# The vector engine's order of work in the last seven routing tiles of a gated attention and mixture-of-experts kernel

## What is computed

```python
x = x + tanh(g_xattn) * attention(layernorm(x), ctx)        # ... @ Wo.T + bo at its end
n = layernorm(x)
shared = (silu(g_s) * y_s) @ w_shared_down                  # g_s, y_s from n @ w_shared_up
scores = sigmoid(n @ w_gate)                                # 64 scores for each token
topk_idx = top 6 of scores; w = their scores, summed to 1
pos = running count of the tokens that chose the same expert before this one
routed = sum over the 6 of w * expert(n), where pos < 512
x = x + tanh(g_ffn) * (shared + routed)
```

## Time and profile before

| | before |
|---|---|
| median of three runs | 3068.83 us (3068.48 to 3069.22) |
| the profiled execution's own time | 3070.04 us |
| span of its trace | 3068.3 us |
| mean granted TensorE clock, as a share of full speed | 0.989 |
| busy: PE, DVE, ACT, POOL | 97%, 72%, 44%, 45% of the span |

### The profile page before, as it was taken

How to read it: one execution, slowest core, us unless ns; L and a number is a source line. 1 busy time by engine, 2 the same in 40 slices (tenths; PEclk the granted TensorE clock), 3 DMA queues, 4 the chain that set the end, 5 groups by cost and what they waited for, 6 DMA issues and landing times.

```text
span 3068.3 us, 62706 instructions
## 1 busy us (share of the span) xinstructions
PE 2981.7 (97%) x21264; PEld 1809.6 (59%) x21264; DVE 2205.3 (72%) x3798; ACT 1352.5 (44%) x2189; POOL 1388.5 (45%) x1325
## 2 busy tenths in 40 slices
PE   6999999999999998999999899999999999999997
PEld 5677777777777764444444445555555555555553
DVE  6677777778787777777777766666666666666664
ACT  5444444444454454111111125555555555555553
POOL 4222222221212213455555745666666665666664
PEclk9999999999999999999999999999999999999998
DMA  5333334333333336444445558999999998999995
GB/s 227 77 94 90 98 95 107 93 87 84 87 87 91 90 103 203 133 136 137 137 136 136 136 178 210 231 249 254 237 244 249 242 244 239 254 260 258 255 259 119
DMA packets 428876, 509.78 MB, mean 166 GB/s; under 512 B 234446, under 2 KB 332750, under 8 KB 428704
## 3 DMA queue, kind: packets, MB, share of 16 engines
q1 hardware_dynamic: 348832, 305.97, 33.3%
q0 software_dynamic: 79872, 201.48, 28.7%
HBM read 340.27 MB, written 201.79 MB: 177 GB/s over the span
## 4 chain that ended last, share of the span: by engine, by line
PE 90%; issue 4%; DVE 2%; POOL 1%; DMA 1%; ACT 0%; SPq 0%; another core or an unknown queue 0%; ACTq 0%; POOLq 0%; DVEq 0%
PE proj_ps L872 7%; PE eturn_ps L2128 7%; PE proj_ps L874 7%; PE proj_ps L873 7%; PE proj_ps L918 4%; PE proj_ps L920 4%; PE proj_ps L919 4%; PE v_ps L2138 3%; PE v_ps L2137 3%; PE v_ps L2139 3%; PE g_ps L2138 3%; PE g_ps L2139 3%; PE g_ps L2137 3%; PE edown_ps L2156 3%; PE edown_ps L2154 3%
## 5 line engine op out<-in xcount | busy, mean ns | idle before, releaser
L1924 POOL DMA_INDIRECT out<-outs,target x256 | 402.2, 1571 | 319.8 <-ACT outs L2015 260.9
L2038 DVE TENSOR_TENSOR ext_lo<-eturn_ps,ext_hi 128x1024 f16<-128x1024 f32 x254 | 311.0, 1224 | 260.9 <-ACT ext_hi L1975 252.3
L1891 POOL DMA_INDIRECT rows<-rows_dram,index x256 | 354.5, 1385 | 118.4 <-POOL index L1887 59.6
L1975 ACT ACTIVATE ext_hi<-eturn_ps 128x1024 f16<-128x1024 f32 x254 | 259.9, 1023 | 216.0 <-PE eturn_ps L2128 155.2
L872 PE MATMUL proj_ps<-ct_hi,wk_wv_hi 128*128 128x256 f16 x1024 | 282.2, 276 | 18.7 <-DVE wk_wv_lo L725 9.5
L872 PE MATMUL proj_ps<-xt,wq_wo_hi 128*128 128x256 f16 x1024 | 279.4, 273 | 5.0 <-DVE whole L701 3.9
L873 PE MATMUL proj_ps<-ct_lo,wk_wv_hi 128*128 128x256 f16 x1024 | 282.0, 275 | 0.0
L874 PE MATMUL proj_ps<-ct_hi,wk_wv_lo 128*128 128x256 f16 x1024 | 281.9, 275 | 0.0
L874 PE MATMUL proj_ps<-xt,wq_wo_lo 128*128 128x256 f16 x1024 | 279.1, 273 | 0.0
L873 PE MATMUL proj_ps<-xt,wq_wo_hi 128*128 128x256 f16 x1024 | 279.1, 273 | 0.0
L2015 ACT ACTIVATE outs<-edown_ps,weight 128x512 f32<-128x512 f32 x256 | 175.8, 687 | 232.0 <-PE edown_ps L2156 224.9
(11 more groups left out here) (216 smaller groups left out, 7319.1 us busy)
## 6 DMA issues: line engine op xcount, KB each, us to landing
ew_in<-w_up SPq DMA_DIRECT2D x64, 1024.0 KB
ew_in<-w_down SPq DMA_DIRECT2D x64, 512.0 KB
x_in<-x SPq DMA_DIRECT2D x16, 1024.0 KB, 5.9
v_dram<-vt SPq DMA_DIRECT2D x64, 256.0 KB, 2.1
late<-v_dram SPq DMA_DIRECT2D x32, 512.0 KB, 7.4
attn_dram<-attn SPq DMA_DIRECT2D x64, 256.0 KB, 2.0
a_in<-attn_dram SPq DMA_DIRECT2D x32, 512.0 KB
rx_in<-x SPq DMA_DIRECT2D x32, 512.0 KB, 4.3
```

The source lines that it names most:

```text
L1891: pool.indirect_dma_start(out=rows[par][:, k, :], out_offset=None, in_=rows_dram, in_offset=bass.IndirectOffsetOnAxis(ap=index[:, par, k:k ...
L1924: pool.indirect_dma_start(out=out, out_offset=bass.IndirectOffsetOnAxis(ap=target[:, k:k + 1], axis=0), in_=outs[:, k, :], in_offset=None, ...
L1975: act.activation(xt_hi[e.base % 2][:, :, k * P:(k + 1) * P], turned_ps(e, k), ACT.Copy).then_inc(xt_hi_made, 1)
L2038: dve.tensor_tensor(xt_lo[e.base % 2][:, :, cols], turned_ps(e, k), xt_hi[e.base % 2][:, :, cols], ALU.subtract).then_inc(xt_lo_made, 1)
```

## The change

In the steps of tiles 25 to 31, DVE normalizes and splits the step's own row ahead of routing the tile before it. All other steps, the other engines' programs and all waits stay as they are.

```diff
             sum_up(t)
+            if is_held(t):
+                norm(t)
+                split_y(t)
             route(t.plus(-1))
-            norm(t)
+            if not is_held(t):
+                norm(t)
             if not is_held(t.plus(-1)):
                 gate_hidden(t.plus(-1))
-            split_y(t)
+            if not is_held(t):
+                split_y(t)
```

## The result

The changed kernel takes 3086.29 us (median of 6, 3085.60 to 3087.51) against 3069.35 for the kernel before on the same chip (median of 6, 3068.48 to 3071.81): the ratio is 1.0057, 95% interval 1.0047 to 1.0067, 14.4 to 20.6 us more. The forecast was 3084.7, with a range from 3076.6 to 3092. The profiled execution took 3086.34 us around a span of 3083.7. One execution of a later run (e5, 4477.15 us at a granted clock of 0.653) was disturbed and is left out of its numbers. As the edit adds five lines, lines behind it are 5 higher: `positions` is L1674, `turn_hidden` L1682, the products L1649 to L1651.

A forecast was written before the change was run, and what follows sets the result against it. Two loops of about 13 us bound the kernel, one through POOL's queue, one through `route` and `gate`. 0.8 + 11.2 - 1.2 + 3.4 + 1.7 = +15.9 us took 3068.83 to 3084.7, range 3076.6 to 3092.

The forecast's parts named there:

- Norm and split earlier, gate's waits gone: DVE's split 6.24 us after y instead of 8.63, so the 8.3 us of `gate` waiting for turned rows go.
- `member` late, PE waiting: `member` ready 9.71 us after y, PE at `positions` after 6.61, so PE stands 3.10 us.
- The loop: From y through `member` and `positions` to the next y: 15.14 us a turn, five turns +11.2 us.
- Step 25: `route` behind the split makes `gate_hidden` of tile 24 late for PE: +0.8 us.
- The tail: Behind y(31), PE turns tile 25's hidden rows at 10.6 us instead of 11.85: -1.2; one clock fall there: +1.7.
- The clock: PE's clock falls behind two of the five new stalls at `positions`, 1.70 us each: +3.4 us.
- The rival in which it falls nearly every time: PE's clock falls at nearly every stall, 8.5 us instead of 3.4 for the five: 3089.8 us; chance 0.15.
- POOL and DVE side by side: POOL, held up while DVE works on rows, has 1.6 us to spare a turn; with full blocking, 0.9 us more.
- The rival on the other side: Turning DMA was the bound, `member` comes by 6.61 us after y: 3064.2 or 3068.4 us; chance 0.11.

The follow-up runs named there:

- e5: Changed kernel with 6 idle products on PE ahead of `positions` in the steps of tiles 27 to 31: median 3079.0 us against 3069.02, ratio 1.0037.
- e1: Changed kernel with only `norm` ahead of `route`, the split back behind it: 3067.84 us against 3067.77 for the kernel before, ratio 1.0002.
- e2: Changed kernel with PE's `positions` a quarter of the product later in the steps of tiles 27 to 31: 3069.17 us against 3067.77, ratio 1.0011.
- e3: Changed kernel with 13 idle products on PE ahead of `positions` in the steps of tiles 27 to 31: 3077.54 us against 3067.77, ratio 1.0034.
- e6: Changed kernel with only `norm` ahead of `route` and `positions` a quarter product later (tiles 27 to 31): 3072.40 us against 3069.02, ratio 1.0008.

## Why the prediction was right

The direction and the mechanism held: PE waits for `member`, and the loop through it sets the turn. The size came out close partly by luck, as the term for the clock was too small and something that has nothing to do with the change made up for it. Step by step:

- **Norm and split earlier, gate's waits gone: right.** Not one wait of `gate` for a turned row is left in the changed kernel's list. (Of the 8.3 us of rows 3, 2.53 lie behind y(31), so the five turns had 5.8 of them.)
- **`member` late, PE waiting: right, to 0.1 us.** I said 9.71 after y and a stall of 3.10. It is 1726.90 + 0.76 = 1727.66, 9.76 after y, and the stall is 3.03 or 3.04 in every turn. That this is the cause is shown, not only read: e1 takes the split out of the string, e2 moves the place where PE needs it, and each returns nearly all of the loss.
- **The loop: 15.14 forecast, 15.27 measured** with the clock held up (e3). Five turns of the string cost 11.9 us against the trace that I had, where I had 11.2.
- **Step 25: right.** +0.8 forecast; y(25) to y(26) is 1664.03 to 1684.17, 20.14 instead of 19.35.
- **The tail: right in its parts.** 10.6 forecast, 10.59 measured; `shared_up(26)` 6.69 instead of 5.34, a fall of 1.35, where I had 1.7. But the gain of 1.2 was that of an execution whose clock fell just there. In the second trace of the kernel before it didn't fall, PE turned the hidden rows 10.40 after y(31), and against that the tail gains nothing.
- **The clock was mis-sized.** I took two falls in five turns at 1.70, +3.4. It was five, 8.2 in all, each 1.5 to 1.7: the second halves took 6.85, 6.99 and three times 7.03 us where 5.34 is the length at full clock. Three gaps of the trace before, of which one of nearly 3 us had no fall, didn't tell how often a stall of 3.03 has one at this place. The rival in which it falls nearly every time, to which I gave 0.15, is the one that happened in this term.
- **Why the total is close all the same.** By the rows of the first pair of traces, 0.8 + 11.9 + 8.2 + the tail's 0.3 make 21.2 us at the end of `shared_up(26)`, five more than forecast. About 5 us of it come off in the expert phase, where the execution that I had in hand had its late load. That is the luck: the load cost 5.3, and I had the falls 4.8 too low. Against the kernel before's second trace the spans differ by 18.7. The medians say 16.9 and, in the second comparison, 16.5; the executions of the kernel before spread over some 10 us, those of the changed kernel over 3. How much of that spread comes from falls and how much from late loads was not settled.
- **POOL and DVE side by side.** POOL's scatters stayed stretched (up to 1.67 against 0.97) and it cost nothing, as POOL has 3.3 to 3.5 us to spare in each turn, and 1.8 still in e3, whose turns are 15.27. The 13.58 that I took for POOL's turn was the longest of three in that trace (the others are 12.95 and 13.08).
- **The rival on the other side**, `member` in time, fell where I had set its point: PE is there 6.6 after y, `member` 3 us later.

## What to carry to other kernels

When a step is moved ahead in one engine's queue, look for the other engine's instruction that reads what is now pushed back, and compare the two arrival times; here 9.7 against 6.6 us decided it. A wait taken away on one result (the turned row, 8.3 us) is no gain if the queue's new order makes another result (`member`, 15 us) later by more. And a stall of TensorE that comes in the same place of every turn may bring a fall of its clock each time: here one of 3.03 us cost 1.4 to 1.7 more, ten times out of ten. As the single gaps of these traces don't say which of them has a fall, the price of "every time" belongs into the range, and a run with the stall filled, like e3, tells the two costs apart.

## What the runs showed of the hardware that I had not expected

- **A stall of 3.03 us in every turn brought the clock down every time**, ten times out of ten in two executions of the changed kernel, though a gap of 2.98 us in the kernel before had no fall, and one of 2.53 had; in its second execution the gap in the place of the 2.53 was 2.61 and had none. Stalls of 1.7 us had none in five (e5), but one of 1.74 in e6 had one, and one of 3.04 there had none. So the length of a single gap doesn't tell in these traces; what does was not found out. After each fall in the changed kernel PE ran at 1.2 GHz for some eight of the 24 products.
- **POOL's addition over 128x1024 holds up small DVE instructions until it ends.** A 128x64 addition took 2.54 us instead of 0.18 (e6). The kernel before has it too, in the steps ahead of tile 26, where its L1501 on 128x6 values takes 2.2 us in each of ten steps, against 0.17 behind them. In each of these it starts 0.13 to 0.23 us behind POOL's addition and ends 0.04 behind it:

```profile
L1501 DVE TENSOR_SCALAR tile<-pos x10: 2189/2253/2269, 1503.6 to 1677.7; 128x6 f32<-128x6 f32 x10
```

  The Trainium skill (SBUF — State Buffer, "Who interferes with whom") says that VectorE (with two inputs in SBUF or in a two-port mode) and GpSimd share a port pair, that whoever issues first has it for the whole instruction, and that the other fully blocks. The ten rows of L1501 agree, though it has one input and no row shows its mode. The two of e6 don't settle the order, as DVE's instructions there start 0.10 and 0.58 us ahead of the addition in the records. In a tight order, where `place` meets `add_bias` can cost 2.4 us or more in a turn; in e6 I had hoped to gain at most 4 in all.
